# Perceiver block on one core: ternary weight pieces moved ahead of a wait, one load moved in SyncE's order, and a key tile's weighting moved by one block

## The reference

```python
x = x + cross_attention(layernorm(x), ctx)     # one head, 512 wide, softmax over 1601 keys
x = x + self_attention(layernorm(x))           # 16 heads of 32, 64 keys, relative position scores
h = gelu(layernorm(x) @ ternary(W1).T + b1)    # 512 -> 2048
x = x + h @ ternary(W2).T + b2                 # 2048 -> 512
```

## Time and profile before

| | |
|---|---|
| median of 3 runs | 626.98 us (624.77 to 629.96) |
| the profiled execution: its own time | 624.94 us |
| its span | 623.2 us |
| mean granted clock of TensorE in it | 0.969 of full |
| busy: TensorE, its weight loads, VectorE, ScalarE, GpSimd | 572.6, 357.5, 419.7, 217.1, 199.0 us |
| HBM read and written | 96.91 MB, 10.49 MB |

### The profile page before, as it was taken

The page is one execution under the profiler, slowest core; times in us unless marked ns, Lnnn a source line. Parts: engine busy times, 40 slices in busy tenths (PEclk is TensorE's granted clock), DMA queues, the critical chain, the costliest instruction groups (busy, mean ns, idle before and its releaser), DMA issues.

```text
span 623.2 us, 13162 instructions
## 1 busy us (share of the span) xinstructions
PE 572.6 (92%) x5237; PEld 357.5 (57%) x5237; DVE 419.7 (67%) x1026; ACT 217.1 (35%) x513; POOL 199.0 (32%) x259
## 2 busy tenths in 40 slices
PE   8999979999999999999885939999999999997887
PEld 7554435444444445446663915866859586684745
DVE  4977399899898988836774282835639284564543
ACT  1221141644545443231231422633616253360502
POOL 0415379798898986800000000101010010101010
PEclk9999999999999999999897969999999999999789
DMA  8980799898999999827340503021020302103000
GB/s 287 367 317 1 266 376 370 299 346 278 393 359 365 349 333 393 309 86 277 136 102 1 159 12 103 18 87 35 39 65 19 102 19 90 32 29 75 18 3 32
DMA packets 58974, 108.26 MB, mean 174 GB/s; under 512 B 19985, under 2 KB 22561, under 8 KB 56865
## 3 DMA queue, kind: packets, MB, share of 16 engines
q1 hardware_dynamic: 58912, 107.41, 49.7%
HBM read 96.91 MB, written 10.49 MB: 172 GB/s over the span
## 4 chain that ended last, share of the span: by engine, by line
issue 37%; PE 34%; DVE 17%; DMA 4%; SPq 4%; POOL 2%; ACT 2%; DVEq 0%; POOLq 0%; ACTq 0%
PE u_ps L909 8%; PE s_ps L883 7%; DVE area L1178 5%; PE u_ps L1050 3%; DMA area<-in_L_xattn_Wo_dram 2%; DVE area L1187 2%; PE max_ps L898 1%; PE s_ps L861 1%; DVE area L1460 1%; SPq L359 1%; PE bank L847 1%; DVE area L1182 1%; PE max_ps L792 1%; DVE s_ps L1288 1%; PE bank L1073 1%
## 5 line engine op out<-in xcount | busy, mean ns | idle before, releaser
L501 POOL TENSOR_SCALAR area<-area 128x384 f32<-128x384 f32 (+1 forms) x160 | 107.4, 685 | 10.3 <-POOL area L494 10.3
L1178 DVE BATCH_NORM_STATS2 area<-area 128x6 f32<-128x384 f32 (+1 forms) x208 | 104.0, 541 | 1.0 <-DMA area<-in_ctx_dram 0.9
L909 PE MATMUL u_ps<-area,yT_all 128*64 128x384 f32 (+1 forms) x416 | 77.4, 497 | 0.9 <-ACT yT_all L623 0.9
L494 POOL TENSOR_TENSOR area<-area,minus_half 128x4 f32<-128x4 f32 (+1 forms) x56 | 59.5, 1062 | 56.6 <-DVE area L1187 56.1
L541 POOL TENSOR_TENSOR area<-area,minus_half 128x1 f32<-128x1 f32 x8 | 4.3, 540 | 221.6 <-DVE area L1454 221.6
L1050 PE MATMUL u_ps<-area 128*128 128x512 f16 x256 | 64.1, 398 | 10.9 <-DVE area L1470 10.9
L883 PE MATMUL s_ps<-area 128*64 128x512 f32 x288 | 66.0, 593 | 0.0
L1050 PEld LDWEIGHTS u_ps<-area 128*128 128x128 f16 x256 | 24.7, 101 | 39.1 <-issue 15.8
L909 PEld LDWEIGHTS u_ps<-area,yT_all 128*64 128x64 f32 (+1 forms) x416 | 25.7, 136 | 29.3 <-issue 27.0
L714 ACT CAST area<-max_ps 128x512 f16<-128x512 f32 x8 | 4.7, 586 | 106.5 <-PE max_ps L1103 106.5
L883 PEld LDWEIGHTS s_ps<-area 128*64 128x64 f32 x288 | 20.4, 137 | 36.5 <-issue 35.7
(11 more groups left out here) (184 smaller groups left out, 1042.2 us busy)
## 6 DMA issues: line engine op xcount, KB each, us to landing
area<-in_ctx_dram SPq DMA_DIRECT2D x96, 384.0 KB, 6.0
area<-in_ctx_turned_dram SPq DMA_DIRECT2D x32, 768.0 KB, 7.0
area<-in_L_ffn_W_turned_dram SPq DMA_DIRECT2D x16, 1024.0 KB, 9.0
skew<-area SPq DMA_DIRECT2D x8, 1024.0 KB, 4.0
area<-skew SPq DMA_DIRECT2D x16, 256.0 KB, 4.7
x_sb<-in_x_dram SPq DMA_DIRECT2D x8, 256.0 KB, 8.5
out_dram<-area SPq DMA_DIRECT2D x8, 256.0 KB, 2.0
area<-in_ctx_dram SPq DMA_DIRECT2D x16, 97.5 KB
```

Source lines behind the costliest of these rows:

```text
L494: pool.tensor_tensor(rs[b][:, sl], ve[b][:, sl], minus_half[:, 0:n], ALU.pow).then_inc(s["rstd_ready"], 1)
L501: pool.tensor_scalar(raw[b][0:m, u, j, :], raw[b][0:m, u, j, :], negmu[b][0:m, i:i + 1], rs[b][0:m, i:i + 1], ALU.add, ALU.mult).then_inc( ...
L909: ins = pe.matmul(u_ps[u * L:(u + 1) * L, 0:DC], pT[0:m, j % NSLOT, u * L:(u + 1) * L], raw[b][0:m, u, j, :], start=(j == 0), stop=(j == N ...
L1178: dve.bn_stats(st[b][0:m, stat_at(u, j), :], raw[b][0:m, u, j, :]).then_inc(s["key_stats_done"], 1)
```

## The change

Three engines' orders are changed; no instruction is added or taken out.

DVE: pieces 2, 3 and 4 stand ahead of the wait for all of `pt_taken`; pieces 5 and 6 take the place of 3 and 4 at the end of dense(0); the calls of 5 in dense(1) and 6 in dense(2) go. Piece 7 stays.

SP: `load_w(6)` goes ahead of `skew_store(0)`; `load_w(7)` stays behind `skew_load(0)`.

PE: `weighted(r, 12)` moves from block 1 to block 0 (2 * NB - 4 is 10 and NJ is 13, so tiles 10, 11 and 12), so ahead of `turn(p, 2)` and `turn(p, 3)`. In dense(0) `xattn_o(1)` moves ahead of the keys' projection. The new form of `att_scores` gives the same call, as LF is 2.

```diff
@@ SP @@
-            load_w(3)
-            load_w(4)
-            load_w(5)
+            for i in range(3, 7):
+                load_w(i)
...
                 if t == 0:
-                    load_w(6)
                     load_w(7)
@@ PE, attention stage @@
-                    if 0 <= r and b < 2:
-                        for j in tiles_of(b + 5):
+                    if 0 <= r and b == 0:
+                        for j in range(2 * NB - 4, NJ):
                             weighted(r, j)
@@ PE, dense stage @@
-                if t == 1:
-                    att_scores(0)
+                if 1 <= t < LF:
+                    att_scores(t - 1)
+                if t == 0:
+                    xattn_o(1)
                 if proj:
                     q_or_k(t, ww, awk, "k_ps", ffn)
-                if t + 1 in AHEAD:
+                if t + 1 in AHEAD and t:
                     xattn_o(t + 1)
@@ DVE @@
+            for i in (2, 3, 4):
+                ternary(i)
             dve.wait_ge(s["pt_taken"], len(PT_USES))
...
-                if t == 0:
-                    ternary(2)
-                if t == LF:
-                    ternary(6)
                 if 1 <= t < NT:
                     softmax_a(t - 1)
                 if t == NT:
                     softmax_b(NT - 1)
-                if t == 1:
-                    ternary(5)
                 if t == LF:
                     ternary(7)
...
                 if t == 0:
-                    ternary(3)
-                    ternary(4)
+                    ternary(5)
+                    ternary(6)
```

## The result

The changed kernel takes 607.47 us (median of 4 runs, 604.4 to 612.59) against 627.03 us for the kernel before on the same chip (4 runs, 624.77 to 629.96). The ratio is 0.9694, with a 95% interval of 0.9616 to 0.9771. The profiled execution took 604.4 us, with a span of 602.6.

A forecast was written before the change was run, and what follows sets the result against it. SP's list, with `skew_store(1)` stuck behind a weight load, was taken to bound the kernel through DVE's late split. Savings of 10.88 + 1.49 + 1.2 = 13.6 us less 1.9 gave 613.2, put at 614.2 us, range 609.5 to 619.5.

The forecast's parts named there:

- 10.88 + 1.49 = 12.37: Step 2: the 10.88 us wait for the gelu split goes, and eight matmuls behind it run 1.49 us faster.
- C: Rival: only part is gained, as a new wait replaces the old, for instance for the skew load; 618.7 us, chance 0.11.
- D: Rival: the skew trip itself, not SP's list, was the bound; 626.6 us, chance 0.04.
- E: Rival: slower, as piece 4's load lands late and delays DVE's queue; 635.5 us at 32 us, chance 0.03.
- the clock in step 1: `att_o(0)` takes 5.45 us or, with the clock up, 3.60; saving 0 to 1.85 us, taken as 0.
- Rival A: The clock stays up in step 1, saving 1.85 us in `att_o(0)` and some 0.2 ahead; 612.1 us, chance 0.18.
- what is saved here should reach the end: Behind step 2's wait: TensorE has almost no gaps, so the 13.6 us saved pass through to the end.
- Tile 12: Attention stage: its four matmuls ahead of `turn(p, 2)` delay ACT's chain; 1.9 us of net loss taken.
- a sign against it: Attention stage: a pair that takes less time than before would show the forecast wrong; no size given.
- rival B: Tile 12 gains: ACT isn't what binds in block 1, and 0.42 us waits go in four pairs; 610.6 us, chance 0.08.

The follow-up runs named there:

- fourth set: Spare transposes added in `z_turn(2)`, far ahead of the tail, to the kernels before and after; tails 51.23 us (after, 14 spares) and 51.47 (before, 24 spares).
- all_warm: The kernel after with spare transposes in TensorE's dense-stage waits and nine more in each wait ahead of `turn_context`; 604.38 us.
- tile12_only: The kernel before with only tile 12 moved to block 0; 0.43%, or 2.7 us, slower than the kernel before.
- pieces_only: The kernel after with tile 12 and `xattn_o(1)` back in their old places; 604.53 and 607.12 us in two sets.

## Why the prediction was wrong

**Right: the block and its price.** SP's list was the bound. Step 2 lost 12.4 us in the profiles where 10.88 + 1.49 = 12.37 were forecast. The skew load was waited for nowhere in step 2, the split was never late, and the store went out at 326.67 (forecast 327). Rivals C, D and E are out.

**Right in kind: step 1.** The turn waited for ACT's copy, as forecast, 1.19 us (forecast 1.2).

**Wrong, first: "I take 0, since the waits still add up to more than half of the stretch."** That is the clock in step 1. The kernel after took 21.05, 23.48 and 21.05 us in three profiles; the forecast comes to 24.46 - 1.2 = 23.26. In two of three `att_o(0)` took 3.67 us. Rival A had this with 0.18, and it came in three of the five profiles with the wait of 1.2 us. It is also no single value: the third profile has 5.89. The reason given for the 0, the sum of the waits, isn't what the profiles sort by; the first wait alone is, slow each time behind 1.84 us or more. The Trainium skill, "TensorE: Matmul & The Clock Gate", section "What's actually happening", by which less idle time speaks for the upper level, pointed the right way in those three of five.

**Wrong, second, and the larger: "After that TensorE runs almost without a gap, so what is saved here should reach the end."** The sum took the stages behind step 2 as fixed. They are the same instructions, but the clock fell at fewer of their waits, and the tail went from 53.97 and 53.96 us to 49.55, 49.56 and 49.61. No term and no end of the range held those 4.4 us, though they could have been suspected: the 3.60 and 3.13 us of a line that takes 1.95 elsewhere stand in the trace of before. The fourth set shows that a few idle matmuls are enough to change the tail; by which way they and the change do it is open.

The three profiled spans of the kernel after have a mean of 605.4 us, and the forecast's span is 613.2 - 1.74 = 611.5. Of the 6.1 us between them the tail is 4.4; step 1 is 23.26 - 21.86 = 1.4; the attention stage is the remaining 0.3: q came at 287.83, 289.39 and 292.24 us in the three, 1.6 later on average than the 288.24 of before, where the forecast had 1.9. That these two agree is partly luck: in the nine profiles of kernels without the move, q came anywhere from 287.85 to 291.21.

**Tile 12: the sign holds, the mechanism in part.** The turn of the context waits 1.67 to 1.73 us for ACT instead of 0.68 (0.73 and 0.77 in two pairs), and the waits for `own_norm` and POOL are gone, as forecast. But where the clock stays up a pair takes 26.84 us instead of 27.05 in the four middle pairs, which the forecast named as a sign against it: one wait in the place of three is a little cheaper. What costs is that the longer wait brings the clock down now and then, some 1.65 us each time. In the eight profiles with the move and without spares in these waits there are eight such pairs in 48; in the nine profiles without the move there are two in 54, of 1.1 and 1.0 us; in `all_warm`, where spares fill these waits, none. That is 1.65 us per execution against 0.2, less the 0.4 us by which q comes earlier where none falls: a loss of some 1.0 us by this count, against 1.9 forecast, and rival B (1.7 gained) is out. `tile12_only` measured 2.7, but its one profile has step 1 at 29.26 us, with the late skew load, so I don't put the whole of it down to tile 12. In the sets where both ran, the kernel without the move was ahead each time, 604.53 to 606.6, 607.12 to 608.46 and (with spares) 607.89 to 608.52, by less than the intervals tell apart.

**Open.** Why the skew load is late in just those runs in which the clock does not fall at the queries, and what decides in one execution whether the clock falls behind a given wait, in the tail too. Whether the change would be as good without tile 12's and `xattn_o`'s part is answered only to half a per cent: not worse.

## What to carry to other kernels

Read the list of an issuing queue as one thread: a load that waits in place for a buffer holds every transfer behind it, however urgent; here moving that one load took 12.6 us out of its own step, and with the shorter tail 16.8 us of 18.4. Give the clock a term of its own in each stage, touched by the change or not: rows of one line and shape that differ in duration (1.95 and 3.60 us here) say where time can come back or be lost when something ahead of them changes. And compare several profiles by stage before a difference of 2 to 5 us is put down to an edit.

## What was not expected of the hardware

A wait of 1.68 us brings the granted clock down in some executions and not in others of the same kernel, with some 1.65 us lost each time. Behind the same wait of 3.27 us in the tail, one row ran slow in one kernel (3.58 us at 557.72) and three in another (3.00, 3.60 and 3.13), though no instruction of that stage differs. Filling waits with spare matmuls left a fall at a later one, `att_o(0)` at 5.37 to 6.01 us in all four kernels with spares for that, and they took 604.38 to 608.52 us, against 604.53 to 608.46 for the kernel after and `pieces_only` without them. And a skew load of 512 KB in two parts took 5.3 to 5.8 us to arrive or 6.2 to 7.4.
